# Building the rotary tables on GpSimd between the second and third sums of the first attention

## The reference

```
h = layernorm(x) * (1 + ca) + sa                      # per batch
q, k, v = h Wq + bq, h Wk + bk, h Wv + bv
qk = q k^T                                            # 512 x 512 for each batch, no heads
theta = 0.5 + 0.2 sigmoid(qk) + 0.15 tanh(qk) + 0.1 relu(qk)
x = x + ga * (softmax(theta) v Wo + bo)
h = layernorm(x) * (1 + cb) + sb
six layers, each of:
    local attention, 16 heads of 64, windows of 32, q and k normalised,
        scaled by q_scale and k_scale, and turned by rotary tables
    feed-forward with gelu gate
x = x + gb * h
```

## Time and profile before

| | us |
|---|---|
| median of 3 runs | 3457.04 (3456.49 to 3458.78) |
| the profiled execution, its own time | 3455.64 |
| its span, first to last instruction | 3453.9 |
| PE busy | 3233.1 (94%) |
| DVE busy | 3171.4 (92%) |
| ACT busy | 2438.2 (71%) |
| POOL busy | 2706.3 (78%) |
| mean granted TensorE clock, as a share of full speed | 0.978 |

### The profile page before, as it was taken

The page is one execution under the profiler, slowest core; times in us unless marked ns, Lnnn a source line. Parts: engine busy times, 40 slices in busy tenths (PEclk is TensorE's granted clock), DMA queues, the critical chain, the costliest instruction groups (busy, mean ns, idle before and its releaser), DMA issues.

```text
span 3453.9 us, 108159 instructions
## 1 busy us (share of the span) xinstructions
PE 3233.1 (94%) x45916; PEld 2089.8 (61%) x46108; DVE 3171.4 (92%) x2914; ACT 2438.2 (71%) x3945; POOL 2706.3 (78%) x1265
## 2 busy tenths in 40 slices
PE   5657999999999999999999999999999999999996
PEld 3325666666666666666666666666666666666663
DVE  6759999999999999999999999999999999999992
ACT  4645777777777777777777777777777777777764
POOL 4547888888888888888878888888888888888871
PEclk9889999999999999999999999999999999999996
DMA  2001111122111122111122111112211122211111
GB/s 77 2 0 32 40 42 39 40 55 57 38 44 39 39 53 57 41 42 42 38 52 54 47 39 41 42 51 52 50 39 40 42 52 51 49 41 39 41 41 39
DMA packets 150433, 148.32 MB, mean 43 GB/s; under 512 B 39228, under 2 KB 95424, under 8 KB 149952
## 3 DMA queue, kind: packets, MB, share of 16 engines
q1 hardware_dynamic: 149952, 141.39, 16.6%
HBM read 19.62 MB, written 2.10 MB: 6 GB/s over the span
## 4 chain that ended last, share of the span: by engine, by line
PE 38%; DVE 26%; ACT 12%; issue 10%; POOL 5%; SPq 2%; DMA 1%; ACTq 0%; DVEq 0%; POOLq 0%
PE bank L574 11%; PE bank L673 7%; DVE rot L1405 6%; PE mid L583 4%; DVE rot L1411 4%; DVE raw L1397 4%; PE mid L624 4%; PE bank L644 4%; DVE Pr L1369 4%; PE mid L611 4%; ACT sq L911 3%; POOL FX L1164 3%; ACT mid L944 3%; DVE mx L1347 2%; ACT raw L903 2%
## 5 line engine op out<-in xcount | busy, mean ns | idle before, releaser
L574 PE MATMUL bank<-wqkv,xs 128*128 128x512 f32 x2304 | 1133.0, 605 | 11.0 <-ACT raw L903 8.5
L1145 POOL TENSOR_TENSOR rr<-ssm,nhalf 128x32 f32<-128x32 f32 x192 | 1051.8, 5478 | 16.0
L1155 POOL TENSOR_TENSOR swp<-raw,TS 128x1024 f32<-128x1024 f32 x384 | 896.8, 2356 | 175.1 <-DVE raw L1397 175.1
L903 ACT ACTIVATE raw<-bank 128x512 f32<-128x512 f32 x768 | 447.5, 598 | 424.2 <-PE bank L574 258.4
L574 PEld LDWEIGHTS bank<-wqkv,xs 128*128 128x128 f32 x2304 | 394.4, 191 | 310.4 <-issue 267.2
L1397 DVE TENSOR_TENSOR raw<-raw,rr 128x2048 f32<-128x2048 f32 x192 | 489.9, 2552 | 16.8 <-POOL rr L1145 16.8
L1391 DVE TENSOR_REDUCE ss<-sq 128x16 f32<-128x1024 f32 x384 | 463.5, 1207 | 23.7 <-ACT sq L911 12.1
L583 PE MATMUL mid<-ident,rot 128*128 128x128 f32 x3072 | 416.6, 279 | 52.0 <-DVE rot L1411 23.1
L583 PEld LDWEIGHTS mid<-ident,rot 128*128 128x128 f32 x3072 | 336.9, 142 | 204.1 <-ACT OT L950 134.6
L1411 DVE TENSOR_TENSOR rot<-rot,swp 128x2048 f32<-128x2048 f32 x192 | 440.1, 2292 | 21.1 <-DVE rot L1405 1.4
L1405 DVE TENSOR_TENSOR rot<-raw,TC 128x2048 f32<-128x2048 f32 x192 | 434.1, 2261 | 0.0
(11 more groups left out here) (134 smaller groups left out, 4443.8 us busy)
## 6 DMA issues: line engine op xcount, KB each, us to landing
PT<-PTd SPq DMA_DIRECT2D x1344, 64.0 KB
xs<-F SPq DMA_DIRECT2D x192, 64.0 KB, 1.9
wqkv<-d_wqkv SPq DMA_DIRECT2D x36, 256.0 KB, 3.3
VT<-V SPq DMA_DIRECT2D x144, 64.0 KB
BT<-PTd SPq DMA_DIRECT2D x288, 32.0 KB
fwo<-d_fwo SPq DMA_DIRECT2D x6, 512.0 KB, 4.1
d_out<-X SPq DMA_DIRECT2D x8, 256.0 KB, 2.3
w<-d_w SPq DMA_DIRECT2D x6, 341.0 KB
```

What stands on the lines that cost most here:

```text
L574: nc.tensor.matmul(bank[bk][:, :], xs[:, j, :], wqkv[:, c, :], start=True, stop=True)\
L903: nc.scalar.activation(raw[:, j % 2, c * 512:(c + 1) * 512], bank[RAW_BANK[c]][:, :], ACT.Copy)\
L1145: pool.tensor_tensor(rr[:, :], ssm[:, :], nhalf[:, :], ALU.pow).then_inc(rr_ready, 1)
L1155: last = pool.tensor_tensor(dst[:, :, :, t, :], src[:, :, :, 1 - t, :], tab.unsqueeze(2).broadcast_to([P, 2, HEADS, 32]), ALU.mult)
```

## The change

In POOL's slot the three tables are built after `theta1` of tile 1 and before `columns(b, 1)` and `theta1` of tiles 2 and 3, where they stood at the end of the slot. The clearing of three buffers in slot 0 moves with them; it is still issued ahead of the tables, and in slot 0 none of the parts that are passed exists, so slot 0 is as before.

```diff
                 part(s, 0, columns, 0)
                 part(s, 3, rstd4, 1)
                 part(s, 1, theta1, 1)
-                part(s, 2, columns, 1)
-                part(s, 1, theta1, 2)
-                part(s, 1, theta1, 3)
                 if s == 0:
                     clear()
                 for i in range(3 * s, 3 * s + 3):
                     if i < DEPTH * TPB:
                         rotary(i // TPB, i % TPB)
+                part(s, 2, columns, 1)
+                part(s, 1, theta1, 2)
+                part(s, 1, theta1, 3)
```

## The result

| us | before | after |
|---|---|---|
| median (lowest to highest), same chip | 3456.76 (3455.52 to 3458.78), 4 runs | 3429.59 (3426.98 to 3430.26), 4 runs |
| ratio, 95% interval | | 0.9919 (0.9907 to 0.993) |
| profiled execution, own time / span | 3455.64 / 3453.9 | 3430.16 / 3428.4 |
| mean granted TensorE clock | 0.978 | 0.984 |
| start of the second stage (first L574) | 223.91 | 197.17 |

A forecast was written before the change was run, and what follows sets the result against it. In the first stage a cyclic chain through several engines, with POOL's three tables on it, sets the period. Gains 13.6 + 5.6 + 1.2 + 7.0 less 0.4 make 27.0 us: 3430.0 us forecast, range 3424 to 3446.

The forecast's parts named there:

- Term a, the wait: DVE's wait for POOL's L1115 before `norm4` at slot ends 1 to 6 goes; 13.6 us gained.
- Term b, `norm4`: DVE's `norm4` no longer runs beside POOL's `theta1` of tile 0, 1.11 us for 2.05; 5.6 us gained.
- The 1.2 us added for L1280: DVE's `theta` of tile 3 no longer runs beside the tables, up to 0.27 us a slot; 1.2 us.
- the rule that the prediction quoted against itself: GpSimd contends with VectorE for SBUF: tables at the new place would move contention, taking back 1.2 us.
- Term c, the clock: TensorE's shorter gap before the last transposes raises its clock through the weighted sum; at most 10.4 us, 7 taken.
- kept a third back: Two thirds of the clock gain taken, since DVE's work behind `norm4` ends only about when the faster weighted sum does.
- The new place: Tables fit POOL's idle time at some 3.66 us; slots 1 and 2 lose 0 to 2 us, 0.4 taken.
- The clock stays: Rival: the wait goes but TensorE's clock still falls behind the shorter gap; 20 us gained, 3437; chance 0.20.
- Another wait takes most: Rival: busy DVE or the moved tables give back 1.5 to 2 us a round; 3446; chance 0.14.
- Slower: Rival: tables at the new place hold the copy of `cur2` and `theta1` of tile 2; 3473; chance 0.03.
- the marks that the prediction named: Signs: L1272 without idle, 1.1 us; PE's wait near 1 us; copy of `cur2` behind ACT; first L574 near 197.
- The period of "about 19 us": Sign: slots 3 to 6 of the first stage take about 19 us each, for 23.7.

The follow-up runs named there:

- experiment 9: Kernel before the change, POOL's `theta1` of tile 0 held until `norm4` and the probabilities of tile 3 are done; 3453.19 us, ratio 0.9988.
- experiment 8: Changed kernel, POOL's `theta1` of tile 1 held until the slot's second `norm4` is done; 3429.81 us.
- experiment 11: Changed kernel, two tables behind `rstd4`, short filling matmuls of 256 and 384 columns, `theta1` of tile 1 held until tile 0's probabilities are written; 3427.6 us.
- experiment 5: Kernel before the change, four filling matmuls of no use ahead of TensorE's last transposes; 3450.6 us, ratio 0.9984.
- experiment 10: Changed kernel, one filling matmul of 256 and one of 384 columns before the transposes of tiles 2 and 3, slots 1 to 7; 3428.94 us.
- experiment 4: Changed kernel, tables of slots 1 to 7 left out and filled with ones instead; 3426.74 us.
- experiment 1: Changed kernel, but one of three tables stays at the slot's end and two are built at the new place; 3430.01 us.
- experiment 7: Changed kernel, but two of three tables stay at the slot's end and one is built at the new place; 3451.49 us.
- experiment 6: Kernel before the change, POOL's `theta1` of tile 0 held until the entering batch's `norm4` is done; 3457.5 us, ratio 0.9998.
- Experiment 2: Changed kernel, but two of three tables built right behind `rstd4`, beside `norm4`, one at the new place; 3430.12 us.

## Why the prediction was right

The forecast was 3430.0 us, measured were 3429.59. The mechanism is the one forecast, and the terms can be followed, though not each by a run of its own. That the totals agree to half a microsecond is in part luck: the runs of after alone spread over 3.3 us, and small misses below cancel.

**Term a, the wait: 13.6 us.** The waits of L1272 fell from 19.8 to 6.2 us, by 13.6. No run takes this wait away alone: wherever it went, the meeting with `theta1` went too, so its worth on the path is only the rest of the sum. Slots 2 to 7 gained 27.0 us; less the 5.8 of experiment 9 and the 7.0 of the clock (below) that leaves 14.2.

**Term b, `norm4`: 5.6 us.** Experiment 9 gives 5.0 us in time and 5.8 in the slots, with some of the clock mixed in. The 1.2 us added for L1280 did not come whole: `theta` of tile 3 takes 0.69 us for 0.93, but `theta` of tile 1 now takes 0.90 beside the tables in slots 3, 4 and 6, for 0.68 (row at 92.88). The 0.66 us that the prediction compared with is a row of tile 2; `theta` of tile 3 undisturbed takes 0.69. Here the rule that the prediction quoted against itself was right in direction. It was not foreseen that the second `norm4` would grow from 1.11 to 2.26 us. In experiment 8 a held `theta1` gives nothing back; experiment 11, without any meeting there, gains 0.2 us a slot.

**Term c, the clock: 7 us of at most 10.4.** The low clock was worth 10.9 us in before (experiment 5) and is still worth 3.85 in after (experiment 10): 7.0 us were won. The prediction got the size right mostly for another reason than it gave, which is luck. It kept a third back because DVE might not keep up. What is in fact missing is for the most part the clock itself, which was low in slots 2, 5 and 7 (weighted sums of 4.78, 4.16 and 3.97 us). In a slot at full clock 2.50 + 0.94 + 0.24 (L1280, 0.69 for 0.93) + 2.04 us (the stretch of PE) = 5.7 us were to be gained, and slots 4 and 6 gained 5.1 and 5.5, so the other engines took back 0.3 to 0.6. DVE is late there, as the prediction feared (PE's wait of 1.23 us for L1303), but it costs little: the stretch is 1.6 us shorter in slot 4 than in slot 5, and the slot is still shorter by 1.1.

**The new place: 0.4 us, and what it could cost.** Table times stayed near the low end (3.58 us for three). In slot 1 the last `theta1` starts at 42.88 for 42.13, 0.75 us late. Against no tables at all the cost is 2.3 us in slots 2 to 7 (experiment 4): more than the 0.4, most of it in slot 2, with the weighted sum there at the low clock again (4.78 us for 3.67). The prediction had put down nothing for that.

**The rivals.** "The clock stays" (3437) held in part, in three of six slots, and cost 3.85 us of the 10.4. "Another wait takes most" (3446) did not come: new waits are there, PE's for ACT and for DVE, but they take back the 0.3 to 0.6 us above and not 1.5 to 2. "Slower" would have needed the copy of `cur2` to be held; it waits for ACT in all of slots 3 to 7.

Of the marks that the prediction named, L1272 without idle time and 1.1 us long, PE's wait near 1 us, the copy behind ACT, and the first L574 near 197 are all there. The period of "about 19 us" is the mean of two kinds of slot, 18.3 and 19.4.

## What to carry to other kernels

Work that nobody waits for belongs where its engine is idle for a later input, not between the last input and the result that another engine needs; find the place in the timeline by who is waited for, and check that the idle time there is longer than the work. One wait on a cyclic path can carry two more losses, the meeting with a long instruction behind it and TensorE's lower clock behind the gap. Neither grows in step with the work that is moved: moving two thirds of the work (experiment 1) brought 23 of 27 us in the slots and moving one third (experiment 7) only 6.5. Before delaying an instruction to avoid a meeting, look at what it meets next.

## What the runs showed of the hardware that was not expected

**DVE is held for the rest of the POOL instruction that it meets.** Where it starts just after a `theta1` of 1.27 us, `norm4` takes 2.05 to 2.30 us for 1.11 and L1293 up to 1.52 for 0.49 (experiments 6 and 8), 0.94 to 1.19 more in each case, a little less than the 1.2 us that the POOL instruction had left; beside tables of 0.32 to 0.50 us, `norm4` takes 1.31. The Trainium skill (SBUF — State Buffer, Who interferes with whom) describes the pair of ports that GpSimd shares with VectorE in its 2-port modes as a lock: whichever of the two issues first has it for its whole instruction, and the other is blocked. The rows beside `theta1` agree with that: of the four instructions of `norm4` one takes 1.28 us and the median 0.33. Experiment 2 fits it too, with 0.49 us for the longest of the four.

**The same gaps give either clock.** In slots 4 and 6 of after the weighted sum runs in 3.67 us, in slots 5 and 7 in 4.16 and 3.97 us, behind idle times of PE that are equal to 0.01 us (0.95 and 0.99). In experiments 4 and 8 slots of 18.1 to 18.2 us and of 19.4 to 19.6 us alternate as well, but there slots 4 and 6 are the long ones. Experiment 10, whose gaps are 0.43 and 0.32 us, has no such slot: every weighted sum takes 3.67 us. What decides in a given slot is open.
